# Reading the bucket numbers of an edge kernel as neighbouring bytes instead of 32-bit words

## What is computed

```python
h = relu(layernorm(x))                    # then, on h:
xn = layernorm(h) * ln_w + ln_b
w_phys   = (silu(rbf @ w1 + b1) @ w2 + b2) * cutoff[:, None]
msg_phys = xn[col] * w_phys
scores   = sum(Q[row] * K[col], per head) / sqrt(32) * cutoff
msg_attn = softmax(scores over the 8 heads) * V[col]
aggr     = segment_sum(msg_phys + gate * msg_attn, row, n)
x + h + aggr @ wo + bo
```

## Time and profile before

| | |
|---|---|
| Time, median of 3 runs | 5557.56 us (5555.09 to 5559.14) |
| Profiled execution | 5559.19 us, span 5557.3 us |
| PE busy in the span | 5156.6 us (93%) |
| DVE busy | 4493.7 us (81%) |
| POOL busy | 4001.3 us (72%) |
| ACT busy | 3260.9 us (59%) |
| Mean granted clock of PE | 0.972 |

### The profile page before, as it was taken

How to read it: one execution, slowest core, us unless ns; L and a number is a source line. 1 busy time by engine, 2 the same in 40 slices (tenths; PEclk the granted TensorE clock), 3 DMA queues, 4 the chain that set the end, 5 groups by cost and what they waited for, 6 DMA issues and landing times. The chain is left out here.

```text
span 5557.3 us, 119878 instructions
## 1 busy us (share of the span) xinstructions
PE 5156.6 (93%) x24352; PEld 3906.9 (70%) x24353; DVE 4493.7 (81%) x11381; ACT 3260.9 (59%) x11609; POOL 4001.3 (72%) x3475
## 2 busy tenths in 40 slices
PE   3879999999999999995899999999999999999999
PEld 3556666666666666674677777777777777777777
DVE  9789887666655555323899999999999999999995
ACT  4223333333333333332788888888888888888884
POOL 1567777777777777775577777777777777777770
PEclk9889999999999999997899999999999999999999
DMA  6234444444444443445999999999999999999965
GB/s 200 89 105 133 144 165 158 142 150 167 158 145 148 168 155 134 152 156 181 314 320 326 325 326 326 325 321 326 325 326 325 326 325 327 324 326 327 326 198 185
DMA packets 584358, 1305.93 MB, mean 235 GB/s; under 512 B 81230, under 2 KB 384118, under 8 KB 582945
## 3 DMA queue, kind: packets, MB, share of 16 engines
q0 software_dynamic: 221536, 881.08, 44.7%
q1 hardware_dynamic: 311780, 345.48, 20.5%
q10 hardware_dynamic: 50850, 77.03, 3.9%
HBM read 1024.15 MB, written 324.38 MB: 243 GB/s over the span
## 5 line engine op out<-in xcount | busy, mean ns | idle before, releaser
L1002 POOL DMA_INDIRECT ukvx<-kvx_table,udst x1760 | 2174.7, 1236 | 668.3 <-issue 480.9
L338 POOL DMA_INDIRECT records<-rows,slot_i x1660 | 1750.9, 1055 | 666.6 <-issue 498.2
L691 PE MATMUL w_ps<-w2s,hid 128*128 128x256 f32 x6656 | 1555.7, 388 | 47.4 <-DVE rows L605 47.3
L691 PEld LDWEIGHTS w_ps<-w2s,hid 128*128 128x128 f32 x6656 | 1251.4, 193 | 371.9 <-issue 156.9
L805 ACT ACTIVATE hid<-hid_ps,b1t 128x512 f32<-128x512 f32 x832 | 525.5, 682 | 1518.5 <-PE hid_ps L680 1504.1
L605 DVE TENSOR_TENSOR rows<-w_ps,b2b 128x512 f32<-128x512 f32 x832 | 570.9, 686 | 749.0 <-PE w_ps L691 748.9
L1118 PE MATMUL ag_ps<-ukvx,uonehot_cut 128*128 128x256 f32 x3520 | 989.3, 404 | 5.3
L1103 PE MATMUL uq_ps<-aggr,uonehotT 128*128 x3520 | 986.4, 404 | 0.0
L1122 PE MATMUL ag_ps<-ukvx,uonehot 128*128 128x256 f32 x3520 | 941.2, 392 | 41.1 <-ACT uonehot L1036 41.1
L1122 PEld LDWEIGHTS ag_ps<-ukvx,uonehot 128*128 128x128 f32 x3520 | 689.0, 196 | 139.7 <-issue 42.2
L1118 PEld LDWEIGHTS ag_ps<-ukvx,uonehot_cut 128*128 128x128 f32 x3520 | 604.8, 192 | 153.9 <-issue 6.3
(11 more groups left out here) (171 smaller groups left out, 5025.0 us busy)
## 6 DMA issues: line engine op xcount, KB each, us to landing
urec<-records SPq DMA_DIRECT2D x880, 260.0 KB
rbf_in<-in_edge_attr SPq DMA_DIRECT2D x207, 256.0 KB, 2.9
kvx_table<-kvx ACTq DMA_DIRECT2D x10, 3456.0 KB, 14.7
ukvx<-kvx_table,udst POOLq DMA_INDIRECT x1760
records<-rows,slot_i POOLq DMA_INDIRECT x1661, 2.6
records<-kvx SPq DMA_DIRECT2D x1, 13000.0 KB
fbase<-x_plus_h SPq DMA_DIRECT2D x14, 896.0 KB, 7.2
out<-fout SPq DMA_DIRECT2D x13, 896.0 KB, 4.9
```

The lines of the kernel that those rows point to most:

```text
L338: pool.indirect_dma_start(recs, bass.IndirectOffsetOnAxis(ap=slot_i[:, q, t:t + 1], axis=0), rows[:, q, t, :], None).then_inc(scattered[q] ...
L691: m = pe.matmul(w_ps[j % 2][:, h, :], hid[:, k % 2, c, h, j * P:(j + 1) * P], w2s[:, c, :], start=(h == 0 and c == 0), stop=(c == 1), skip ...
L1002: pool.indirect_dma_start(kvx[:, k, j, :], None, table, bass.IndirectOffsetOnAxis(ap=dst_i[:, k, j:j + 1], axis=0), bounds_check=NPAD - 1, ...
```

## The change

The table `half_bucket` becomes one of bytes (`U8`) instead of 32-bit integers, 1824 bytes a partition instead of 7104. PE's load of a turn reads 32 neighbouring bytes where it read 27 words. ACT's reads 16 neighbouring bytes, from the even position on, where it read 8 words with a step of two, and `keep` takes the odd ones of them. Behind the loops both read 16 bytes. The zeros behind the table grow from 9 to 57 elements. On all five engines the instructions stand in the same order as before, in the same number; only the width of that one fill and the loads themselves differ. The memory behind the table moves down by 5280 bytes.

```diff
+U8 = mybir.dt.uint8
+SEEN = 32
...
-        half_bucket = sb("half_bucket", [1, HALVES + 2 * DEPTH], I32)
+        half_bucket = sb("half_bucket", [1, HALVES + 2 * SEEN], U8)
...
-            bucket_of = [None] * DEPTH
+            bucket_of = [None] * (2 * DEPTH)
...
                 if k == 0:
                     _, bucket_of[:] = nc.values_load_multi_w_load_instructions(
-                        (half_bucket[0:1, 1:2 * DEPTH + 1] if first else half_bucket[0:1, bass.ds(u * 2 + 1, 2 * DEPTH)]).rearrange("a (k j) -> a k j", j=2)[:, :, 0],
+                        half_bucket[0:1, 0:2 * DEPTH] if first else half_bucket[0:1, bass.ds(u * 2, 2 * DEPTH)],
                         engines=[mybir.EngineType.Activation], min_val=0, max_val=BUCKETS - 1,
...
-                    keep(u - LAG, bucket_of[k])
+                    keep(u - LAG, bucket_of[2 * k + 1])
...
-            _, rest = nc.values_load_multi_w_load_instructions(half_bucket[0:1, HALVES + 1:HALVES + 2 * LAG], engines=[mybir.EngineType.Activation], min_val=0, max_val=BUCKETS - 1,
+            _, rest = nc.values_load_multi_w_load_instructions(half_bucket[0:1, HALVES:HALVES + 2 * DEPTH], engines=[mybir.EngineType.Activation], min_val=0, max_val=BUCKETS - 1,
...
-                keep(UNITS - LAG + n, rest[2 * n])
+                keep(UNITS - LAG + n, rest[2 * n + 1])
...
-            SEEN = 2 * (DEPTH + LAG + ASK_AHEAD - 1) + 3
             near = [None] * SEEN
...
-            _, rest = nc.values_load_multi_w_load_instructions(half_bucket[0:1, HALVES:HALVES + HLAG], engines=[mybir.EngineType.PE], min_val=0, max_val=BUCKETS - 1,
+            _, rest = nc.values_load_multi_w_load_instructions(half_bucket[0:1, HALVES:HALVES + 2 * DEPTH], engines=[mybir.EngineType.PE], min_val=0, max_val=BUCKETS - 1,
```

## The result

The changed kernel takes 6125.33 us (median of 4 runs, 6125.23 to 6126.76), the kernel before 5557.38: ratio 1.1023, 95% interval 1.1004 to 1.1042. The profiled execution took 6126.76 us with a span of 6124.8, 567.5 more than before. The forecast was 5526.

A forecast was written before the change was run, and what follows sets the result against it. DVE was taken to bound the kernel at 3.131 us a unit, losing 33.5 us, mainly waiting for PE. Waits of 22.9 us and most of 10.6 behind them give 31: 5557.6 − 31, forecast 5526 us, range 5518 to 5578.

The forecast's parts named there:

- What bounds the kernel: DVE sets the pace at 3.131 us a unit; 33.5 us are lost, mostly in 45 waits for PE's queries.
- the forecast's own term: DVE's 22.9 us of waits for PE and most of the 10.6 us behind them go: 31 us won.
- no change of the clock: PE's clock may go on falling after idle time; no gain or loss was counted for this.
- PE's lead: Behind its load PE is 1.09 us ahead; a clock fall costs 1.70, leaving 0.61 uncovered, so loads under 1.74 end waits.
- The price of the load: PE's load of 32 bytes, at 12 ns a register and 13 a byte passed over, takes 1.42 us instead of 2.35.
- fixed part: Share of a load's time independent of its length: 618 ns on PE, 797 ns on ACT.
- The upper bound of 4.33 us: PE's load if each of 32 bytes is one slow read of 116 ns on top of 618 ns.
- The rule of 200 ns a register: Skill's price for bulk loads, which would put PE's load at 6.4 us; not borne out by 87 ns at most.
- Each byte is a slow read of its own: Rival: PE's load takes 4.33 us and PE becomes the bound, 5670 to 5860 us; chance 0.05.
- By registers: Rival: load cost goes by register count, PE's load 2.67 us, time 5572 to 5592, best guess 5574; chance 0.15.
- the gathers become slower: Rival: tiles at other addresses slow the gathers, 27 us for each per cent beyond 5% slack; chance 0.03.
- ACT's load: ACT's load falls from 1.73 to 1.20 us, winning nothing; growth covered up to 0.75 us, at 2.65 costing 20 us.

The follow-up runs named there:

- words_28_b: Kernel before with 28 instead of 27 neighbouring words in PE's load: 5534.95 us, ratio 0.9957; words_28, the same kernel on a slower chip: 0.9883.
- packed_words_b: Changed kernel, bytes read as words (8 PE, 4 ACT), numbers taken out by shift and mask: 5527.21 us, 0.9944 to before; packed_words, on a slower chip: 0.9986.
- words_32_16: Changed kernel with its table in 32-bit words again, PE reading 32 and ACT 16 neighbouring words: ratio 0.9939 to the kernel before, repeated 0.9946.
- shift_96: Kernel before with 96 unused bytes behind its table, moving the tiles behind it to the changed kernel's remainder of 256 bytes: ratio 1.0002.
- packed_pe_bytes_act_b: Changed kernel with PE's 32 bytes read as 8 words and ACT still loading 16 single bytes: 5641.99 us, ratio 1.0147 to the kernel before.

## Why the prediction was wrong

**What bounds the kernel: right.** DVE at 3.131 us a unit, 33.5 us to win, PE late behind its load when the clock falls. words_28_b, whose load is 0.47 us shorter, gained some 23 us of time; packed_words_b gained 31, which is the forecast's own term. But I had counted on no change of the clock, and in packed_words_b the falls themselves are gone. So its 31 us don't test whether DVE would have been free of the falls, and the equal number is in part luck.

**PE's lead: right.** I had 0.61 us missing at each fall, so a load below 1.74 us would end the waits. With a load of 1.88 the same query still comes 0.15 us late on average at 32 falls, and 0.61 − 0.47 = 0.14.

**The price of the load: the step that failed.** "The new load on PE: 618 + 32 × 12 + 32 × 13 = 1.42 us." It measured 7.56: on PE 235 ns for each byte, where I had 12 for a register and 13 for a byte passed over. Three things in it were wrong.
- ACT's load behind the loops reads 5 neighbouring words (`HALVES + 1` to `HALVES + 5`, of which three are used), not 3 with a step of two, as the text ahead of the prediction and the prediction have it. So ACT's slope was not 581 / 5 = 116 but 581 / 3 = 194 ns, and 1726 / 8 = 216: single elements at some 210 ns, in plain sight.
- PE's 27 and 7 words both have a remainder of three by fours. The difference of the two hides just the part that costs most, 3 × 235 ns, and puts it into a "fixed part" of 618.
- With two unknowns and two slopes every pair of slopes is explained. I called that the only reading that explains both by one cause.

The upper bound of 4.33 us, one slow read for each byte, rested on the same 116 ns. With 235, and no fixed part, it is 7.5, and the range would have had to reach 6100. Nor is there a fixed part of 618 ns in a load: PE's 8 words take 592 in all, ACT's 4 words 310.

**The rule of 200 ns a register.** The Trainium skill, "Runtime: NRT & Kernel Launch" (section on instruction fetch mechanics), gives about 200 ns a register for a bulk load; it speaks there of the loads that the runtime puts in. I set it aside because PE's 27 words took 87 ns each. The changed kernel's loads are 7557 / 32 = 236 ns an element on PE and 3392 / 16 = 212 on ACT: they lie 18% and 6% above it. It does not hold for aligned words in fours, 64 ns each.

**The rivals.** "Each byte is a slow read of its own" was the case, with a chance of 0.05, but at twice the price that I gave it, so the time lies far above its 5670 to 5860 too. Its formula, with the measured load, gives 8 × 2.87 + (0.76 + 5.21) + 0.4 = 29.3 and the fall's 1.5 us, 30.8 us a turn; measured 30.7. "By registers" is refuted by words_32_16, "the gathers become slower" by packed_words_b and shift_96.

**ACT's load.** I held it for covered up to 0.75 us. packed_pe_bytes_act_b bears that out (0.8 us of the surplus of 1.67 reach DVE). The size was wrong by the same slope: 2.65 us was the upper bound, 3.39 measured, and 115 us are its price where PE's load is short.

## What to carry to other kernels

In these runs a load into registers is priced neither by bytes nor by registers: count how many groups of four aligned 32-bit words it has (257 ns each on PE), and how many elements are left over (235 ns each). Round the count up to fours, start on a multiple of 16 bytes, and if numbers are packed narrower, read them as words and shift. Before a price is fitted from a few rows, look up in the code what each row reads, and give the rival in which each element is its own transfer the price of the dearest row. A single instruction in an engine's sequencer can be the longest stop of the array in a loop, and no busy time shows it. And a wait that is gone from a list of waits may only have become short: compare the starts with the ends that they depend on.

## What the runs showed that I had not expected

- 27 neighbouring words take 2.35 us, 28 take 1.88 and 32 take 2.14. One word more made the kernel 0.43% faster.
- Bytes and 16-bit numbers cost the same an element (7557 and 7544 ns for 32).
- With the gap at 1.1 us the granted clock stayed at 1.00; with 1.74 it fell in some turns, with 5.96 in each.
- On chips 5 and 13 the kernel before took 600 us longer, prep too (from 1000 to 1400 us, in a part that words_28 leaves as it was, PE is busy for 365 of 400 us on chip 13, and for 395 in the first trace). The profile of words_28 puts some waits in prep down to "remote", which the first trace never names. What they are stays open, and so does why the 28 words gained 1.2% there and packed_words nothing.
